# One layer of KL attention and gated feed-forward on 8 cores: p goes through DRAM and transposing loads instead of TensorE, its row sums are folded into the second matmul, and the statistics of tiles 8 to 15 move to VectorE

## The reference

```python
xn = _layernorm(x, axis=-1)
# attention
logp = jax.nn.log_softmax(xn, axis=-1)
p = jnp.exp(logp)
cross = jnp.einsum('bid,bjd->bij', p, logp)
kl = jnp.sum(p * logp, axis=-1)[:, :, None] - cross
attn = jax.nn.softmax(-kl, axis=-1)
att = jnp.einsum('bij,bjd->bid', attn, xn)
# feed-forward, D = 1024, H = 3072
h = jax.nn.silu(xn @ wg.T) * (xn @ wu.T)
out = x + att + h @ wd.T
```

## Time and profile before

| what | us |
|---|---|
| median of 3 executions | 861.68 |
| lowest and highest | 861.22, 918.38 |
| the profiled execution's own time | 861.79 |
| its span, from the first to the last instruction of core 7 | 860.2 |
| TensorE busy in the span | 756.8 (88%) |
| VectorE busy | 259.3 (30%) |
| ScalarE busy | 220.3 (26%) |

### The profile page before, as it was taken

One profiled execution on the slowest core, in us unless ns is written; L12 is line 12 of the kernel. 1 busy time (PEld: TensorE's weight loads), 2 busy tenths in 40 slices (PEclk: granted clock), 3 DMA queues, 4 the chain that ended last, 5 costly groups with the idle time before them and its releaser, 6 DMA issues.

```text
span 860.2 us, 9408 instructions; the slowest of 8 cores (856.7 to 860.2 us)
## 1 busy us (share of the span) xinstructions
PE 756.8 (88%) x3840; PEld 355.4 (41%) x3840; DVE 259.3 (30%) x292; ACT 220.3 (26%) x269; POOL 12.7 (1%) x25
## 2 busy tenths in 40 slices
PE   0024679999999999999999999999999999999997
PEld 0024434444444444444444444444444444444443
DVE  4347421100101102112721272136113712361136
ACT  1888753051150240122012201210121022102210
POOL 5000000000000000000000000000000000000000
PEclk9996689999999999999999999999999999999999
DMA  8999999992000013550320132013201320000027
GB/s 238 227 116 104 113 109 112 109 115 34 1 0 2 0 29 71 108 88 19 79 50 0 26 73 50 0 33 66 50 1 38 61 49 1 0 2 0 1 97 294
DMA packets 82889, 55.17 MB, mean 64 GB/s; under 512 B 78160, under 2 KB 78160, under 8 KB 82272
## 3 DMA queue, kind: packets, MB, share of 16 engines
q0 software_dynamic: 2976, 27.30, 23.0%
q1 hardware_dynamic: 79872, 27.28, 13.8%
HBM read 46.17 MB, written 27.26 MB: 85 GB/s over the span
## 4 chain that ended last, share of the span: by engine, by line
PE 86%; ACT 7%; issue 3%; DMA 2%; DVE 2%; POOL 0%; ACTq 0%; DVEq 0%; POOLq 0%
PE ps L186 12%; PE ps L626 10%; PE ps L641 10%; PE ps L629 10%; PE ps L638 10%; PE ps L698 10%; PE ps L701 9%; PE ps L469 7%; PE ps L471 6%; DMA x_sb<-x 2%; PE ps_bf L359 1%; ACT ps L259 1%; ACT xnT L300 1%; ACT L238 1%; ACT scr L655 1%
## 5 line engine op out<-in xcount | busy, mean ns | idle before, releaser
L698 PE MATMUL ps<-arena 128*128 128x512 bf16 x384 | 145.5, 379 | 8.8 <-ACT scr L655 4.6
L626 PE MATMUL ps<-xnT,arena 128*128 128x512 bf16 x384 | 145.5, 379 | 1.8 <-DVE x_sb L484 1.8
L638 PE MATMUL ps<-xnT,arena 128*128 128x512 bf16 x384 | 145.5, 379 | 0.0
L641 PE MATMUL ps<-xnT,arena 128*128 128x512 bf16 x384 | 145.5, 379 | 0.0
L629 PE MATMUL ps<-xnT,arena 128*128 128x512 bf16 x384 | 145.5, 379 | 0.0
L701 PE MATMUL ps<-arena 128*128 128x512 bf16 x384 | 145.5, 379 | 0.0
L669 DVE TENSOR_TENSOR arena<-scr,ps 128x1024 bf16<-128x1024 f32 x48 | 58.6, 1221 | 281.8 <-ACT scr L655 281.8
L710 DVE SCALAR_TENSOR_TENSOR x_sb<-ps,x_sb 128x1024 f32<-128x1024 f32 x96 | 117.6, 1225 | 51.0 <-PE ps L701 50.7
L186 PE MATMUL ps<-arena,xnT 128*128 128x512 bf16 x512 | 114.9, 387 | 4.7 <-ACT arena L206 4.7
L655 ACT ACT_TABLE_LOAD x24 | 30.8, 1283 | 319.6 <-PE ps L641 319.6
L469 PE MATMUL ps<-arena 128*128 128x512 bf16 x256 | 96.3, 376 | 5.7 <-ACT arena L206 4.5
(11 more groups left out here) (55 smaller groups left out, 413.5 us busy)
## 6 DMA issues: line engine op xcount, KB each, us to landing
x_sb<-x POOLq DMA_DIRECT2D x8, 1024.0 KB, 17.0
o<-x_sb SPq DMA_DIRECT2D x16, 512.0 KB, 2.7
wg_bf<-wg POOLq DMA_DIRECT2D x4, 1536.0 KB, 81.7
wu_bf<-wu POOLq DMA_DIRECT2D x4, 1536.0 KB, 95.3
wd_bf<-wd POOLq DMA_DIRECT2D x4, 1536.0 KB, 171.1
arena<-wg_bf SPq DMA_TRANSPOSE x48, 2.9
arena<-wu_bf SPq DMA_TRANSPOSE x48, 2.9
arena<-wd_bf SPq DMA_TRANSPOSE x24, 4.1
```

The source lines that it names most:

```text
L626: te.matmul(base[:, 0:512], lg, xnT_sl(dc, th * 1024, 512), start=st_, stop=sp_)
L638: te.matmul(base[:, 1024:1536], lu, xnT_sl(dc, th * 1024, 512), start=st_, stop=sp_)
L641: ins = te.matmul(base[:, 1536:2048], lu, xnT_sl(dc, th * 1024 + 512, 512), start=st_, stop=sp_)
L698: te.matmul(ps03[:, q5 * 1024: q5 * 1024 + 512], lh, wdT_sl(b2, hcb * 1024, 512), start=st_, stop=sp_)
```

## The change

p no longer goes through TensorE and PSUM. VectorE writes p as before into ptile; SP stores each tile to a DRAM tensor p_dram (semaphores pa0 and pa1, for even and odd tiles), and after every fourth tile, once the stores are complete, issues eight transposing loads of 512 x 128 into pT (semaphore t0g for tiles 0 to 3, tg for the other three groups together). pcast(t) waits for the store of tile t-2. M1(0) waits for t0g, M1(1) for all of tg.

The bias -ln s_j is gone. The bf16 xn goes into a buffer of its own (xnb, four tiles) for TensorE's transposes, and VectorE writes xn times 1/s_j into xntok (the step that the text calls xnw) and 1/s_j into rs_bf, which takes the place of the column of ones. The M1 evacuation is exp without bias, and both Ln activations with their negations are gone.

Pass 1 of tiles 8 to 15 is on VectorE, two tiles at each of k = 0 to 3, ahead of the casts; ScalarE's Square and Copy activations and emit_conv are gone. Pass 2 of tiles 0 to 7 comes first on ScalarE, that of tiles 8 to 11 at k = 1, of 12 to 15 at k = 3.

```diff
+    p_dram = nc.dram_tensor("p_dram", [T, D], BF16, kind="Internal").ap()
+    p_r = p_dram.rearrange("(t p) d -> p t d", p=128)
...
+        xnb = sb("xnb", [128, 4 * D], BF16)
+        rs_bf = sb("rs_bf", [128, NT], BF16)
...
                 if p < 2:
-                    wt(te, E[("pTe", sg * 4 + 3)])
+                    if sg == 0:
+                        wt(te, ("t0g", 128))
+                    else:
+                        wt(te, ("tg", 384))
...
-                            AF.Exp, bias=st_neglse[:, jc:jc + 1])
+                            AF.Exp)
...
-            emit_pass2(0)
-            emit_pass2(1)
-
-            @block.scalar
-            def _(a):
-                trash = ps47[:, 0:1024]
-                ev = None
-                for t in range(8, 16):
-                    wt(a, E[("xq8", t // 2)])
-                    wt(a, ev)
-                    e1 = mark(a.activation(trash, xs(t), AF.Square,
-                                           accum_out=st_sq[:, t:t + 1]), "ac")
-                    wt(a, e1)
-                    E[("p1a", t)] = ev = mark(
-                        a.activation(trash, xs(t), AF.Copy,
-                                     accum_out=st_sum[:, t:t + 1]), "ac")
-
-            emit_pass2(2)
-            emit_pass2(3)
+            for pr in range(4):
+                emit_pass2(pr)
...
                     wt(v, e3)
+                    wt(v, E.get(("xnTr", t - 4)))
                     E[("xncast", t)] = mark(
-                        v.tensor_copy(out=xntok_sl(t, 0, D),
+                        v.tensor_copy(out=xnb[:, tq * D:(tq + 1) * D],
                                       in_=xn32), "dv")
...
-                    wt(v, E.get(("ptr", t - 2)))
+                    if t >= 2:
+                        wt(v, ("pa%d" % (t % 2), 16 * ((t - 2) // 2 + 1)))
                     e32 = scr32[:, tq * D:(tq + 1) * D]
                     E[("pcast", t)] = mark(v.tensor_scalar(
                         out=ptile[:, q * D:(q + 1) * D], in0=e32,
                         scalar1=st_rs[:, q:q + 1], scalar2=None,
                         op0=ALU.mult), "dv")
-                    if t >= 1 and with_pte:
...
+                    mark(v.tensor_copy(out=rs_bf[:, t:t + 1],
+                                       in_=st_rs[:, q:q + 1]), "dv")
+                    E[("xnw", t)] = mark(v.tensor_scalar(
+                        out=xntok_sl(t, 0, D),
+                        in0=xnb[:, tq * D:(tq + 1) * D],
+                        scalar1=st_rs[:, q:q + 1], scalar2=None,
+                        op0=ALU.mult), "dv")
+
+            def emit_p_store(t):
+                @block.sync
+                def _(sy, t=t):
+                    wt(sy, E[("pcast", t)])
+                    q = t % 2
+                    mark(sy.dma_start(out=p_r[:, t, :],
+                                      in_=ptile[:, q * D:(q + 1) * D]),
+                         "pa%d" % (t % 2), 16)
+                if t % 4 == 3:
+                    g = t // 4
+                    @block.sync
+                    def _(sy, g=g):
+                        thr = 32 * (g + 1)
+                        sy.wait_ge(sems["pa0"], thr)
+                        sy.wait_ge(sems["pa1"], thr)
+                        sm = "t0g" if g == 0 else "tg"
+                        for dc in range(NDC):
+                            mark(sy.dma_start(
+                                out=pT_sl(dc, g * 512, 512),
+                                in_=p_dram[g * 512:(g + 1) * 512,
+                                           dc * 128:(dc + 1) * 128],
+                                transpose=True), sm, 16)
...
             def emit_pe_transp(t):
                 emit_pe_transp_xn(t)
-                emit_pe_transp_p(t)
+                emit_p_store(t)
...
-                    if k == 0:
-                        emit_conv(8)
-                        emit_pass2(4)
-                        emit_pass2(5)
-                    if k == 2:
-                        emit_conv(12)
-                        emit_pass2(6)
-                        emit_pass2(7)
+                    if k < 4:
+                        emit_pass1(8 + 2 * k)
+                        emit_pass1(9 + 2 * k)
+                        if k == 1:
+                            emit_pass2(4)
+                            emit_pass2(5)
+                        if k == 3:
+                            emit_pass2(6)
+                            emit_pass2(7)
...
-                            ins = te.matmul(den, lhsT, ones_bf[:, :],
+                            ins = te.matmul(den, lhsT,
+                                            rs_bf[:, jc:jc + 1],
                                             start=st_, stop=sp_)
...
-            emit_pe_transp_p(12)
-            emit_pe_transp_p(13)
```

More of the change, by code:

```diff
@@ L77, in build_nc @@
         s_li = ctx.enter_context(nc.semaphore("li"))
+        s_pa0 = ctx.enter_context(nc.semaphore("pa0"))
+        s_pa1 = ctx.enter_context(nc.semaphore("pa1"))
+        s_t0g = ctx.enter_context(nc.semaphore("t0g"))
+        s_tg = ctx.enter_context(nc.semaphore("tg"))
         s_g0 = ctx.enter_context(nc.semaphore("g0"))
@@ L337, in _ @@
                         op0=ALU.mult), "dv")
-                    if t >= 1 and with_pte:
[L339 to L346, removed]
-                        E[("pTe", t - 1)] = mark(
-                            v.tensor_copy(out=dstp, in_=srcp), "dv")
+                    mark(v.tensor_copy(out=rs_bf[:, t:t + 1],
[27 more added lines that the diff above has]
+                                transpose=True), sm, 16)
             def emit_pe_transp_xn(t):
@@ L361, in _ @@
                                   q * 1024 + dc * 128 + 128],
-                            xntok_sl(t, dc * 128, 128), sb_id[:, :])
+                            xnb[:, tq * D + dc * 128: tq * D + dc * 128 + 128],
+                            sb_id[:, :])
                     E[("xnTr", t)] = mark(ins, "pe")
-            def emit_pe_transp_p(t):
-                @block.tensor
-                def _(te, t=t):
-                    q = t % 2
-                    wt(te, E[("pcast", t)])
-                    wt(te, E.get(("pTe", t - 2)))
-                    for dc in range(NDC):
-                        ins = te.transpose(
-                            ps_bf[:, 2048 + q * 1024 + dc * 128:
-                                  2048 + q * 1024 + dc * 128 + 128],
-                            ptile[:, q * D + dc * 128: q * D + dc * 128 + 128],
-                            sb_id[:, :])
-                    E[("ptr", t)] = mark(ins, "pe")
             def emit_pe_transp(t):
                 emit_pe_transp_xn(t)
-                emit_pe_transp_p(t)
+                emit_p_store(t)
             emit_dve_pre(0)
@@ L432, in _ @@
                 wt(a, E[("xnTr", NT - 1)])
-                wt(a, E[("exp", 11)])
                 emit_xnTe(a, NT - 2)
                 emit_xnTe(a, NT - 1)
-                E["lnsA"] = mark(a.activation(
-                    st_lns[:, 0:12], st_s[:, 0:12], AF.Ln), "ac")
-            @block.vector
-            def _(v):
-                wt(v, E["lnsA"])
-                E["nlsA"] = mark(v.tensor_scalar(
-                    out=st_neglse[:, 0:12], in0=st_lns[:, 0:12],
-                    scalar1=-1.0, scalar2=None, op0=ALU.mult), "dv")
         with nc.psum_tensor("ps03", [128, 2048], F32) as ps03:
@@ L462, in _ @@
                             wt(te, E[("xnTe", NT - 1)])
-                            wt(te, E[("pTe", NT - 1)])
+                            wt(te, E[("xnw", NT - 1)])
                             wt(te, E["consts"])
@@ L501, in _ @@
                                      accum_out=st_s[:, t:t + 1]), "ac")
-                wt(a, E[("exp", 15)])
-                E["lnsB"] = mark(a.activation(
-                    st_lns[:, 12:16], st_s[:, 12:16], AF.Ln), "ac")
-            @block.vector
-            def _(v):
-                wt(v, E["lnsB"])
-                E["nlsB"] = mark(v.tensor_scalar(
-                    out=st_neglse[:, 12:16], in0=st_lns[:, 12:16],
-                    scalar1=-1.0, scalar2=None, op0=ALU.mult), "dv")
-            emit_dve_post(12, with_pte=True)
-            emit_dve_post(13, with_pte=False)
+            emit_dve_post(12)
+            emit_p_store(12)
+            emit_dve_post(13)
+            emit_p_store(13)
             for p in range(4):
@@ L519, in build_nc @@
                     emit_m1_evac(0, [p - 1, p])
-            emit_pe_transp_p(12)
-            emit_pe_transp_p(13)
-            @block.vector
-            def _(v):
-                for t in (12, 13):
-                    qp = t % 2
-                    wt(v, E[("ptr", t)])
-                    dstp = arena[:, PT0:PT0 + NDC * T].rearrange(
-                        "p (dc t) -> p dc t", dc=NDC)[
-                        :, :, t * 128:(t + 1) * 128]
-                    srcp = ps_bf[:, 2048 + qp * 1024: 2048 + (qp + 1) * 1024
```

(23 more changed lines are left out.)

37 lines of the change are left out of this document (3 added, 34 removed).

## The result

The changed kernel takes 998.31 us (median of 9 runs) against 861.61 (median of 10): the ratio is 1.1583, 95% interval 1.1571 to 1.1596. It is slower by 137 us, in the direction and nearly by the size of the main case (997). In some executions of most kernels here the cores of one die are slower, at a lower granted clock: ratios compare only the other executions, single times are of those, and medians are over all.

What follows compares the result with a forecast made beforehand. Until 171 us the start of M1(0) and M2(0) bounds the kernel, then matmuls alone. With SP's transfers waiting behind the weight copies, between +125 and +140: 861.8 + 135 = 997 us, range 843 to 1008.

Steps and rivals of the forecast that it cites:

- main case: SP's stores and loads beside the weight copies: each packet waits for a 4.8 us copy packet; +135 us, 997 us; chance 0.42.
- One sign: On VectorE, as a mark of being right: its largest wait would be pcast on a p_dram store.
- Statistics: Tiles 8 to 15, ScalarE to VectorE: exp(0) ends near 29 us instead of 50.4; VectorE takes over 12.7 us.
- xnw and the small copy: VectorE's added work per tile: xnw taken as 0.5 us (bounds 0.15 and 0.81), the small copy 0.1 us.
- Turns: DMA engines, 36 to 203 us: 35 turns of 4.8 us, so only stores 0 to 3 get through before the copies end.
- M1(0), 249 forecast: Start of the first query group's M1 on TensorE: near 249 us instead of 102.6, +146 us.
- M1(0) to M2(0): Stretch of 39.0 us, 6 off: p transposes 1.7, wait for L560 1.20, two Ln with table loads 2 x 1.5.
- one-packet end: SP gets one packet per engine turn beside the copies: +146 at M1(0), less 6 inside, +140 us.
- bunches of 17: SP gets about 17 packets per engine turn: stores come early, group 0's packets fill the queue; +125 us.
- A whole DMA per turn: First rival, DMA engines: 28 turns of some 5.5 us before M1(0), M1(0) near 195; +92, 954 us; chance 0.18.
- one wait per burst: Rival: SP's queue goes first after the current copy packet; stores land in 7.5 us, M1(0) about 100, 853 us; chance 0.15.
- No delay: Rival: DMA engines serve SP at once; M1(0) at 92, 10.6 + 6 = 17 us saved, 845 us; chance 0.25.

Runs made afterwards that it cites:

- e1: Changed kernel with GpSimd's twelve weight copies issued only once all of p's transposing loads have landed: median 844.04 us, ratio 0.9789.
- e9: Kernel before with the weight copies issued only once xnT is complete, nothing else edited: ratio 0.9995.
- e5: Kernel before with only the statistics of tiles 8 to 15 moved to VectorE in the loop; p on TensorE, bias and Ln as before: ratio 0.9807.
- e6: Kernel before with five small SP transfers beside the weight copies, each issued once the one before has landed, nothing on the path waiting: 860.4 us, one run.
- e2: Changed kernel with p again transposed on TensorE and copied out of PSUM by VectorE, the rest of the change kept: ratio 0.9813, about 846 us.
- e3_packets_16k: Changed kernel with the same weight copies cut into smaller transfers, 128 rows of gate and up, 32 of down: 1000.21 us in one run.

## Why the prediction was right

**The order of the argument held:** the copies' share of 1.00 and their uncut 4.8 us packets were enough to see that SP's traffic would be held up until about 203 us, and that 16 tiles' work in order behind pcast carries it to M1(0). e1 and e9 show that both are needed: the copies, and something beside them. One sign was off: over the whole span pcast's wait for p_dram, 163.0 us in all, is not VectorE's largest (two waits of later stages are longer), only the largest ahead of M1(0).

**Statistics.** exp(0) was put at an end near 29 us; it runs from 27.56:

```profile
27.56 1.06 ACT L372 ACTIVATE scr<-scr 128x1024 f32<-128x1024 f32 x1
```

e5 gives this part's worth by itself: 17 us. It is not the 21 us by which exp(0) is earlier, because VectorE took the statistics over.

**xnw and the small copy.** Estimated 0.5 and 0.1 us, measured 0.48 and 0.15. The evacuation without bias, which I had costed at nothing, is shorter, 595 ns instead of 684; how much of the 1.3 us behind M2(0) (717.3 against 718.6) that makes was not isolated:

```profile
L208 ACT ACTIVATE arena<-ps 128x512 bf16<-128x512 f32 x64 | 34.6, 595 | 16.2 <-PE ps L192 16.1
...
L304 DVE TENSOR_SCALAR arena<-xnb,st_rs 128x1024 bf16<-128x1024 bf16 x16 | 7.6, 477 | 0.0
```

**Turns, a term that was mis-sized.** "From 36 to 203 us there are 167 / 4.8 = 35 turns: stores 0 to 3 are all that gets through before the copies end." Stores 0 to 3 were through at 168.5 us: 36 packets in 135 us, 3.75 us each and not 4.8, because the copies' completions give a turn too (e6). It didn't matter for the sum, since group 0's 272 packets per engine then filled the queue until the copies ended; store 4 was issued at 212.3 (forecast 215), pcast(6) came at 215.9 (218), pcast(11) at 235.0 (238). Which of the two ends, 1 packet or a bunch per turn, was right was left open in the prediction: e6, and the 439 and 437 packets above, settle it for one.

**M1(0), 249 forecast, 243.9 measured.** 3 us are the above; 2 us are the distance from pcast(11) to M1(0), 8.9 us instead of the 10.9 of the kernel before. 0.75 of them VectorE gains up to its last cast, without the copy of p out of PSUM and the wait for it. The other 1.3 are behind the last cast: 4.5 us to M1(0) instead of 5.7. The p transposes aren't the reason, as e2 has them and takes 4.5 too; in the kernel before, tiles 12 and 13 are still in TensorE's transposes when the last cast ends, so two rounds of transposes and ScalarE's copies are left, and here one.

**M1(0) to M2(0), 33 forecast, 35.9 measured: the term that was wrong by half.** I took 6 us off, 3.1 were there. Of p's part, forecast at 2.9, e2 (37.2, with p on TensorE) leaves 1.3: the transposes are gone, but where M2(0) waited 1.20 us for L560 it now waits 1.65 for an evacuation. Of Ln and the bias, forecast at 3, e5 (39.05, with them) against e2 leaves 1.9, and not by the way forecast. The two Ln bring no table load of their own. The kernel before, on ScalarE:

```profile
111.91 0.20 ACT L503 ACTIVATE st_lns<-st_s 128x4 f32<-128x4 f32 x1
112.13 1.28 ACT L206 ACT_TABLE_LOAD   x1
```

and the changed kernel, which still has that load:

```profile
253.00 1.28 ACT L208 ACT_TABLE_LOAD   x1
```

So the matmuls go on behind the first evacuation only 0.6 us sooner (11.6 us after M1(0) in e2, 12.3 in e5). The other 1.2 us is TensorE's granted clock. The next 32 matmuls, in the kernel before (e5 has 9.83 us and 0.70 as well) and in e2:

```profile
114.84:124.61 9.77, 9.77 (x32) 3.84 (x33) 0.18 (x1) 3.56 (x5) 0.00 (x0) 0.70 0.99 107
```

```profile
101.33:109.92 8.59, 8.59 (x32) 3.50 (x33) 0.00 (x0) 3.21 (x5) 0.00 (x0) 0.80 1.06 118
```

At the full clock 32 take 27.66 / 4 = 6.9 us. A granted clock of 0.70 or 0.80 is the mean of a stretch partly at the lower of the two levels, 1.2 and 2.4 GHz. Ahead of it TensorE had stood for 4.68 us before and 3.47 in e2; what set the clock was not tried.

**The sum.** +141.3 - 3.1 = 138.2 us at M2(0), and 136.9 at the end of the span, against the 140 of the one-packet end. The forecast had M1(0) 5 us too late and the stretch behind it 3 us too short, which leaves 2, and 1.3 came behind M2(0). The 997 stood 5 us under the one-packet end for another reason, because I split the difference with bunches of 17, which e6 refutes. That the two fell together, so that 997 met 998, is luck; the mechanism is not, and the one-packet end by itself, 1002, would have been 3.5 us off.

**From queue to queue.** In e6 SP's queue started one row, of 256 B or of 2 KB, for each packet of the copy queue. The Trainium skill, page "DMA: Bandwidth & Descriptors", section "Queues, rings and completion order", tells of a round by packets, and with that the trace agrees; the 9 to 17 descriptors that it gives for a packet are not what SP's stores did here, and the measurement decides. The prediction laid that rule to the whole of +125 to +140; a store in one turn is not the one-packet end.

**The rivals.** A whole DMA per turn (954 us) and one wait per burst (853) fall by e6: 8 rows cost more than 4, and 4 more than 1. No delay (845) is what e1 gives, 844.04, so its sum holds for a kernel whose copies are elsewhere, though by two errors that cancel: M1(0) came at 89.2 and not 92, the stretch behind it is 3.1 us shorter and not 6. The 954 of the first rival has a slip: it leaves out the 6 us inside that the other sums take off, and would have been 948.

## What to carry to other kernels

Before putting a transfer on the path, look at what the DMA engines do at that time: here, at a share of 1.00 made of few, large packets, every small packet of another queue waited for a packet of theirs (3.7 us on the mean), and the price went by the number of packets per engine, with some 12 us for the transfer, and not by bytes or by the landing time on idle engines. Background copies with slack belong behind such transfers; here that took one wait and was worth 154 us. And take a change apart before judging it: one part of this one gives all of its 2% gain, and another hides it under a loss nine times as large (998 against 844 us).

## What the runs showed of the hardware that was not expected

- The tiny packets of the copy queue, by their number its completions, take a turn like any other: 32 starts of SP's queue against 16 large and 16 tiny ones of the copy queue in 2.5 us (e6), and 437 against 439 in 100 us of the changed kernel.
- Every transfer beside the copies pays some 12 us however small it is: one packet per engine landed in 15.4 us, against 2.7 us for 512 KB on idle engines. About 6 us of it pass before the first packet starts; the rest, its completion's turn among it, was not taken apart.
- The issue itself can stand. SP's issue of a transposing load takes 1.2 us on idle engines; with three loads already in the queue it took 33.47 us in the changed kernel, and 75.88 us in e3_packets_16k, and all that SP had behind it stood too.
